# Order within a step of the two GCN rounds: relu ahead of the scale pass on ACT, the next half's scaled sums ahead of one-hots and statistics on DVE

## What is computed

```python
def gcn_conv(x, edge_index, edge_weight, W, b, improved_fill=2.0):
    xw = x @ W
    ...
    norm = dinv[row] * ew * dinv[col]
    agg = jax.ops.segment_sum(xw[row] * norm[:, None], col, num_segments=n)
    return agg + b
h = gcn_conv(x, edge_index, edge_weight, W1, b1)
h = layer_norm(jax.nn.relu(h), g1, be1)
h = h + jax.nn.relu(t @ Wt + bt)
h = gcn_conv(h, edge_index, edge_weight, W2, b2)
h = layer_norm(jax.nn.relu(h), g2, be2)
# the caller: x = _layernorm(x + gcn(x))
```

## Time and profile before

| | us |
|---|---|
| median of 3 runs | 6518.18 (6513.54 to 6526.69) |
| the profiled execution | 6529.06 |
| its span | 6527.2 |
| PE, DVE, ACT, POOL busy | 4735.7, 3273.3, 2416.2, 1918.4 |

### The profile page before, as it was taken

The page is one execution under the profiler, slowest core; times in us unless marked ns, Lnnn a source line. Parts: engine busy times, 40 slices in busy tenths (PEclk is TensorE's granted clock), DMA queues, the critical chain, the costliest instruction groups (busy, mean ns, idle before and its releaser), DMA issues. The chain is left out here.

```text
span 6527.2 us, 120714 instructions
## 1 busy us (share of the span) xinstructions
PE 4735.7 (73%) x23954; PEld 3001.6 (46%) x23955; DVE 3273.3 (50%) x10024; ACT 2416.2 (37%) x4967; POOL 1918.4 (29%) x1886
## 2 busy tenths in 40 slices
PE   5887677566868888756665776775888876777776
PEld 3553443233335555344442443433666644656552
DVE  4443343456444454456664666664444433555564
ACT  2342332344247776345542444442222221222222
POOL 5531760643033331064402433102223202222210
PEclk9998899788779999877787778887999998888887
DMA  4552663454234443244432444332333322333322
GB/s 132 176 167 95 203 204 123 143 163 155 84 95 143 142 145 126 86 135 138 135 114 78 142 133 133 124 111 73 112 102 103 108 96 80 96 92 98 92 82 83
DMA packets 429789, 789.70 MB, mean 121 GB/s; under 512 B 69303, under 2 KB 75250, under 8 KB 429716
## 3 DMA queue, kind: packets, MB, share of 16 engines
q1 hardware_dynamic: 375060, 671.58, 30.8%
q0 software_dynamic: 54656, 117.32, 7.4%
HBM read 480.10 MB, written 308.53 MB: 121 GB/s over the span
## 5 line engine op out<-in xcount | busy, mean ns | idle before, releaser
L1033 PE MATMUL p_agg<-onehot,msg 128*128 128x512 f16 (+1 forms) x2384 | 1046.1, 439 | 1028.6 <-DVE onehot L1430 624.0
L627 POOL DMA_INDIRECT raw<-node_s,src_i x980 | 962.1, 982 | 2036.3 <-DMA node_s<-o 855.5
L1430 DVE TENSOR_SCALAR onehot<-iota,dst_f,negbase 128x512 f16<-128x512 f16 (+1 forms) x2384 | 970.8, 443 | 972.8 <-PE p_agg L1035 470.7
L1035 PE MATMUL p_agg<-onehot,msg 128*128 128x512 f16 (+1 forms) x2384 | 1055.6, 443 | 0.0
L1033 PEld LDWEIGHTS p_agg<-onehot,msg 128*128 x2384 | 240.5, 101 | 1533.3 <-issue 1470.0
L1421 DVE TENSOR_TENSOR msg<-raw,msg x140 | 180.4, 1289 | 685.1 <-ACT msg L748 643.4
L1479 DVE BATCH_NORM_STATS2 stats<-v_ring 128x6 f32 (+1 forms) x1960 | 426.9, 281 | 187.0 <-ACT v_ring L826 135.1
L627 POOL DMA_INDIRECT raw<-node_x,src_i x392 | 379.4, 968 | 458.0 <-issue 445.4
L818 ACT ACTIVATE o<-v_ring,nmr,rstd 128x128 f32 (+1 forms) x1176 | 472.2, 483 | 101.5 <-DVE nmr L1495 95.1
L1408 DVE SCALAR_TENSOR_TENSOR hid<-type_in,p_wide 128x512 f32<-128x512 f32 x448 | 251.1, 616 | 321.1 <-PE p_wide L1013 235.3
L788 ACT ACTIVATE u<-p_agg,sage_bias 128x512 f32<-128x512 f32 x196 | 133.9, 683 | 703.8 <-PE p_agg L1064 703.4
(11 more groups left out here) (252 smaller groups left out, 7977.2 us busy)
## 6 DMA issues: line engine op xcount, KB each, us to landing
node_s<-o SPq DMA_DIRECT2D x392, 256.0 KB
feature<-u SPq DMA_DIRECT2D x294, 256.0 KB, 2.1
h_in<-feature SPq DMA_DIRECT2D x294, 256.0 KB
node_x<-o SPq DMA_DIRECT2D x294, 256.0 KB
res_in<-node_x SPq DMA_DIRECT2D x294, 256.0 KB, 3.2
h_in<-node_x SPq DMA_DIRECT2D x196, 256.0 KB
h_in<-node_s SPq DMA_DIRECT2D x196, 256.0 KB
h_t<-dinv_scratch SPq DMA_DIRECT2D x196, 256.0 KB, 3.8
```

The lines of the kernel that those rows point to most:

```text
L627: nc.gpsimd.indirect_dma_start(out=raw[:, (e % RING) * BATCH + j, :], out_offset=None, in_=src_d, in_offset=bass.IndirectOffsetOnAxis(ap=s ...
L1033: nc.tensor.matmul(p_agg[:, a, :], tile_ap(msg, t, 0, D), oh, start=first, stop=True, skip_group_check=True)
L1035: return nc.tensor.matmul(p_agg[:, a, :], tile_ap(msg, t, D, 2 * D), oh, start=False, stop=True, skip_group_check=True)
L1430: return V.tensor_scalar(tile_ap(onehot, slot), iota[:, :], dst_f[:, bass.ds(t, 1)], negbase[:, bass.ds(it * 2 + a, 1)], ALU.subtract, ALU ...
```

## The change

It changes the order of calls at two places and adds or takes away no instruction.

```diff
@@ ACT, step(it) of the GCN rounds
                     if k >= 4:
                         relu_out(it - 1, 1)
                         deviation(it - 1)
+                        relu_out(it, 0)
                         if k == 4:
                             scale_rows(it - 2)
                         else:
                             second_deviation(it - 2)
-                        relu_out(it, 0)
                         normalise_rows(it - 1)
                         if k == 5:
                             second_normalise(it - 2)
@@ DVE, gcn_step(it)
                     scaled_sums(it, 1)
                     statistics(it - 1, 1)
                     gain_and_shift(it - 2)
+                    scaled_sums(it + 1, 0)
                     if exists(it + 1):
                         onehots(it + 1, 1, after)
                     scale_and_move(it - 1)
                     statistics(it, 0)
-                    scaled_sums(it + 1, 0)
                     if k == 5:
                         second_scale_and_move(it - 2)
```

## The result

| | before | after |
|---|---|---|
| median | 6520.87 us (6513.54 to 6533.84) | 6546.28 us (6540.9 to 6557.04) |
| the profiled execution | 6529.06 | 6550.71 |
| its span | 6527.2 | 6548.9 |

The ratio is 1.0041, with a 95% interval of 1.003 to 1.0051. The kernel became slower by 0.4%, and the median lies 0.3 us above the forecast's upper end of 6546. The forecast of 6529 was counted from a median before of 6518.18 over three runs; over nine runs it is 6520.87, so 2.7 us of the distance are no part of the change. The spans of the two profiled executions differ by 21.7 us, where 10.9 were forecast. Where they are is read from the starts of L1518, the gain, one a step. The steps between two gains fall into edge steps (25), plain steps (12) and the eleven without a batch at the end.

The account below looks back on a forecast made before the run. No engine is full; chains through the engines bound the steps, ACT's in first-round edge steps, DVE and ACT's through `nmr` in the second. Terms -35 + 22.2 + 10.0 + 13.7 = +10.9 us on 6518.18 gave 6529, range 6500 to 6546.

Parts of the forecast that it names:

- Second round: Second GCN round: sums ahead of `nmr` cost time, and POOL's multiply holds DVE operations; +44.7 us between its gains.
- The 0.60 a step: Second GCN round: sums put ahead of `nmr` on the chain lengthen 29 light steps by 0.6 each, 17.4 us.
- the nine that were to absorb it: Second-round steps whose one-hots already meet POOL's multiply; the sums stand in that gap, so their 0.6 is free.
- 7 + 5 steps: Second round: the multiply holds `nmr` in seven steps (1.96 each, 13.7 us) and a third one-hot in five (10.0 us).
- Rivals 1: Second round: first come, first served, so the seven small operations pass the multiply; -3, 6515 us; chance 0.22.
- 3: Second round: POOL's multiply gets out of DVE's way, so neither the 13.7 nor the 10.0; 6505 us; chance 0.13.
- 4: Second round: the sums' 0.6 is hidden and nothing is held; -35, 6483 us; chance 0.05.
- Relu ahead of the scale, edge steps: First GCN round: the relu leaves ACT's chain, scale to norm falls from 2.83 to 2.55 us in 25 steps; gain 7.0.
- Plain steps: First GCN round: DVE's 2.59 us wait for the relu goes in 12 steps, 156.0 us becoming 134.4; gain 21.6.
- Last eleven steps: End of the first GCN round, steps without a batch: idle ahead of the statistics shrinks in four; gain 6 us.
- Rival 2: PE is late for the moved sums, delaying DVE's one-hots and lists in 16 steps; +25, 6543 us; chance 0.15.
- The forecast's bound for the first round: First GCN round: gain of 35 us forecast, at least 22 (half of the plain steps' gain) and at most 42.

Follow-up runs that it names:

- sums_alone: Only the sums' move on DVE, in both GCN rounds, against the kernel before; ACT keeps its old order: 6569.93 us, ratio 1.0077.
- list_early: The changed kernel, with ACT in the first GCN round reading the next list of batches ahead of the norm's wait for the scale: 6546.8 us.
- nmr_ahead: Kernel before plus the relu's move, and in the second GCN round `nmr` on DVE ahead of the second half's one-hots: 6475.79 us, ratio 0.9938.
- root_between: norm_and_list, with ACT's second root between the norm's sixth and seventh instructions and L1542, L1544 right behind the one-hots, second round: 6384.08 us, ratio 0.9793.
- norm_and_list: Relu's move, early list in first round; in the second, `nmr` behind the residual sum and ACT's norm ahead of the second root: 6430.48 us, ratio 0.9859.

## Why the prediction was wrong

The mechanisms were right in the round that loses and mis-sized in the round that wins.

**Second round: right.** +44.7 was forecast between its gains and +42.9 came. The 0.60 a step was 0.47 to 0.62 in the steps where nothing holds (0.89 in one); of the nine that were to absorb it eight did (0.0 each; their one-hots now take 2.2 us instead of 2.8, in one 2.6 instead of 3.2) and one half (0.3); 7 + 5 steps were held for 2.56 to 2.59 each, against 0.6 + 1.96 and 0.6 + 2.0. The mean `nmr` rose to 0.48 us. The first step won 1.2, which the forecast doesn't have: its one-hots meet a multiply too, and this one came 1.25 earlier behind the gain. The pair without the multiply shows that the +2.0 in these 12 steps is the multiply. Rivals 1, 3 and 4 fell with this: the seven `nmr` were held (1), the multiply did not give way (3), and the 0.6 was paid (4). The sums' move without the relu's cost nearly the same, +41.1, so the relu has no part in it that is seen.

**Relu ahead of the scale, edge steps: the failed step.** This term of 7.0 us came to nothing. The forecast took "2.83 us now" against "2.55 us" as a gain, 25 x 0.28 = 7.0. Two terms were missing. Scale to norm is 2.64 and not 2.55: the row came from the end of the round, outside the loop over pairs, and there it is 2.55 after as well; inside the loop the norm starts 0.20 behind the end of the scale. Why the two differ was not tried. And `msg`, the instruction behind the norm, does not follow the engine but the sequencer, which lost the relu as cover. The steps came out 0.3 us longer; with the list read early they are 5.8 us shorter than that.

**Plain steps: right in kind, 21.6 forecast and 17.1 measured.** The steps that meet the multiply came to 11.29 to 11.46 (forecast 11.4). Those whose multiply is out of the way came to 11.1 to 11.2 instead of 10.9. The same two terms on ACT have a share in this: in the kernels with the relu's move and ACT's early list and the sums in their old place, such steps take 11.0. The rest is in the steps with a third one-hot, forecast at 11.2 to 11.4: 11.73, 11.32, 12.68 and 12.20, and in the first plain step, 11.99. The forecast's "reading of the lists and one-hots 3.52" was read where the sums still stood ahead of the reading and covered part of it. Without them the idle time ahead of these one-hots is 2.6 to 3.45 us instead of 2.0 to 2.7; with the relu alone, where the sums still cover it, it is 2.3 to 2.65. The step of 12.68 has a second multiply, 8.12 behind the gain, as well.

**Last eleven steps: 6 forecast, 1.7 measured.** The relu alone won 4.9 there. The other 3.2 are missing with both moves, where the forecast had the sums' move at nothing ("in the first round the move costs nothing on the ACT chain"). How much of this is DVE's list behind the sums' move and how much PE's lower clock, 0.85 against 0.89, is open.

**Rival 2** gave 6543, near the measured time, for a reason that did not occur: the wait of L1506 for PE in the first round is 1.8 us in two steps. A rival's number is no evidence for it.

The misses in the first round add up to 16.1 us: 7.3 in the edge steps, 4.5 in the plain ones, 4.3 in the last eleven. Between the rounds 0.5 more are missing; the second round cost 1.8 less than forecast, and the ends of the span are 4.0 shorter, of which no run tells the cause. That makes the 10.8 between the 10.9 forecast and the 21.7 of the profiled executions. The medians lie 25.4 apart, 3.7 more than these two executions; with the 2.7 of the median before, that is the distance from 6529 to 6546.28. The forecast's bound for the first round was a gain of 22 at least, and 18.5 came, because the edge steps' 7.0 had been given no lower end: a chain that runs through an engine was priced by the engine's rows alone.

## What to carry to other kernels

An instruction on a chain may cost nothing because the sequencer reads lists or hands over the next ones beside it. Before counting its removal as a gain, look at what the same engine issues next, and whether that start follows the end of the work ahead of it or the release of a wait. A move that is good in one round of a shared step function should be priced in the other by the question which small result the other engine waits for; here it was `nmr`, and the kernel that moves it forward, with ACT's norm and root arranged around it and the first round's part kept, is 2.1% (1.9 to 2.2) faster where the change lost 0.4%. Where two engines hold each other up, the place of a 0.17 us instruction matters to half a microsecond: 0.62 us ahead of the multiply it took 2.35 us, 0.66 ahead it took 0.17. Before a difference in steps that PE paces is put down to an order, the granted clock of both stretches is to be compared.

## What the runs showed of the hardware

- A POOL TENSOR_TENSOR over SBUF holds some DVE instructions that start up to 0.6 us ahead of its own recorded start, until 1.7 us behind that start (multiply of 1.69). SCALAR_TENSOR_TENSOR on 128x8 with both inputs in SBUF was held when it began 0.36 to 0.62 us ahead (0.17 us became 2.09 to 2.35, 37 times in `after`, `sums_alone`, `list_early`, `nmr_ahead` and `root_between`) and not when it began 0.66 us ahead or more. By the Trainium skill (SBUF — State Buffer, section "SBUF: two separate sides", on the shared pair) whoever starts first has the pair for the whole instruction. That agrees only if the multiply takes the pair some 0.65 us ahead of the start that the profile gives; the runs here can't tell this from another order.
- RECIPROCAL with one input was not held. L1542 began 0.2 to 1.3 us behind the start of a multiply in the kernels before, `nmr_ahead` and `norm_and_list`, 32 times, and took 0.19 to 0.20 us each time; L1544 right behind it lasted until the multiply's end, as in the earlier trace rows. The sums, with one input in PSUM, ran beside it too: begun 0.4 us ahead of the multiply to 1.0 behind it, they took 0.66 to 0.68. The same page of the Trainium skill counts DVE operations with two SBUF inputs among those that contend, and the trace agrees.
- An ACT instruction that waits for the ACT instruction ahead of it started 0.20 us behind its end, 40 times in the first round of the changed kernel.
- In this loop, from the start of ACT's norm to `msg` it is 3.30 us on the mean of 25 edge steps when nothing else covers the reading of the list, 3.11 with the relu ahead of the norm, and 3.09 when the list is read early; on DVE the reading shows as 2.0 to 3.5 us of "issue".
